# The hand-written schedule of a state-space mixer with a mixture of experts: x's scaling and z one unit later, x's stores earlier in the queue, and a new order inside chunk 0

## What is computed

```python
def layernorm(x): return (x - mean(x)) / sqrt(var(x) + 1e-5)

u  = layernorm(x)                                  # 16 x 512 x 128
h  = causal_convolution(u @ B_w.T, powers of eig)  # 64 states, |eig| = 1
x  = x + layernorm(h @ C_w.T + D * u)              # the mixer
t  = layernorm(x)
cw = softmax(t @ w_router) * softmax(t @ w_gating / 0.1); cw /= sum(cw) + 1e-9
o  = sum over 8 experts e of cw[e] * ((silu(t @ w_gate[e]) * (t @ w_up[e])) @ w_down[e])
x  = x + layernorm(o)
```

## Time and profile before

| | us |
|---|---|
| median of 3 runs | 1149.61 (1148.16 to 1149.87) |
| the profiled execution | 1147.37 |
| its span, first to last instruction | 1145.4 |
| PE busy | 1110.9 (97%) |
| DVE busy | 936.1 (82%) |
| ACT busy | 731.6 (64%) |
| POOL busy | 708.5 (62%) |
| TensorE clock granted, mean | 0.997 |

### The profile page before, as it was taken

How to read it: one execution, slowest core, us unless ns; L and a number is a source line. 1 busy time by engine, 2 the same in 40 slices (tenths; PEclk the granted TensorE clock), 3 DMA queues, 4 the chain that set the end, 5 groups by cost and what they waited for, 6 DMA issues and landing times.

```text
span 1145.4 us, 16858 instructions
## 1 busy us (share of the span) xinstructions
PE 1110.9 (97%) x4818; PEld 897.2 (78%) x4818; DVE 936.1 (82%) x1751; ACT 731.6 (64%) x1415; POOL 708.5 (62%) x900
## 2 busy tenths in 40 slices
PE   8998999999999999999999999999999999999997
PEld 4676787787877878787887877878777887888885
DVE  7778888787888978888887887978878887887865
ACT  6765666656666576666656666576666756666564
POOL 1587766648557475766748567575756748557453
PEclk9999999999999999999999999999999999999998
DMA  4430322213132222322213133222322313132110
GB/s 137 118 111 12 100 56 77 72 47 93 47 93 75 65 65 50 99 56 77 72 48 98 42 93 74 66 65 54 95 56 76 73 47 93 46 84 56 43 52 19
DMA packets 184588, 80.17 MB, mean 70 GB/s; under 512 B 126736, under 2 KB 162224, under 8 KB 184496
## 3 DMA queue, kind: packets, MB, share of 16 engines
q1 hardware_dynamic: 184496, 79.09, 26.2%
HBM read 59.40 MB, written 19.66 MB: 69 GB/s over the span
## 4 chain that ended last, share of the span: by engine, by line
PE 73%; POOL 14%; issue 7%; ACT 1%; DVE 1%; POOLq 0%; ACTq 0%; DVEq 0%
PE y L365 8%; PE g L367 8%; PE g L365 8%; PE g L366 8%; PE y L367 8%; PE y L366 8%; PE u L365 8%; PE u L367 7%; PE u L366 7%; POOL hid_lo L1285 6%; POOL acc L1292 2%; POOL mv L1236 1%; POOL rstd L1250 1%; ACT hid_hi L673 1%; PE m_ps L365 1%
## 5 line engine op out<-in xcount | busy, mean ns | idle before, releaser
L1285 POOL TENSOR_TENSOR hid_lo<-hid,hid_hi 128x512 fp32r<-128x512 f32 x255 | 335.3, 1315 | 363.5 <-ACT hid_hi L673 363.4
L983 DVE TENSOR_TENSOR hid<-gate,u 128x512 f32<-128x512 f32 x512 | 348.9, 682 | 188.6 <-ACT gate L667 163.9
L667 ACT ACTIVATE gate<-g 128x512 f32<-128x512 f32 x512 | 305.2, 596 | 299.2 <-PE g L367 298.9
L673 ACT ACTIVATE hid_hi<-hid 128x512 fp32r<-128x512 f32 x512 | 319.8, 625 | 38.3 <-DVE hid L983 36.4
L989 DVE TENSOR_TENSOR hid_lo<-hid,hid_hi 128x512 fp32r<-128x512 f32 x257 | 236.7, 921 | 0.1
L365 PE MATMUL y<-hid_hi,w_hi 128*128 128x512 f32 x512 | 201.6, 394 | 12.2 <-POOL hid_lo L1285 11.6
L365 PE MATMUL g<-xe_hi,w_hi 128*128 128x512 f32 x512 | 200.2, 391 | 4.5 <-POOL w_lo L1228 2.9
L365 PE MATMUL u<-xe_hi,w_hi 128*128 128x512 f32 x512 | 200.0, 391 | 2.4 <-DVE hid L983 2.4
L367 PE MATMUL g<-xe_hi,w_lo 128*128 128x512 f32 x512 | 199.4, 389 | 0.0
L367 PE MATMUL u<-xe_hi,w_lo 128*128 128x512 f32 x512 | 199.4, 389 | 0.0
L367 PE MATMUL y<-hid_hi,w_lo 128*128 128x512 f32 x512 | 199.4, 389 | 0.0
(11 more groups left out here) (223 smaller groups left out, 1165.1 us busy)
## 6 DMA issues: line engine op xcount, KB each, us to landing
cw_b<-cw_scratch SPq DMA_DIRECT2D x128, 256.0 KB, 3.4
x_sb<-x_in SPq DMA_DIRECT2D x16, 256.0 KB, 3.1
xn_scratch<-mix_t SPq DMA_DIRECT2D x60, 64.0 KB, 2.7
feat<-xn_scratch SPq DMA_DIRECT2D x15, 256.0 KB, 2.6
out_scratch<-acc_t SPq DMA_DIRECT2D x60, 64.0 KB, 1.9
ffn<-out_scratch SPq DMA_DIRECT2D x15, 256.0 KB, 2.7
x_out<-o_sb SPq DMA_DIRECT2D x15, 256.0 KB, 2.4
y_scratch<-mix_t SPq DMA_DIRECT2D x56, 64.0 KB, 1.9
```

Of the source, the lines that this page charges most:

```text
L667: nc.scalar.activation(gate[:, k % 2, :], g_ps[k % 2][:], ACT.Silu).then_inc(gate_ready, 1)
L673: nc.scalar.activation(hid_hi[:, k % RING, :], hid[:, k % RING, :], ACT.Copy).then_inc(hi_ready, 1)
L983: nc.vector.tensor_tensor(hid[:, k % RING, :], gate[:, k % 2, :], u_ps[k % 2][:], ALU.mult).then_inc(hid_ready, 1)
L1285: nc.gpsimd.tensor_tensor(hid_lo[:, k % RING, :], hid[:, k % RING, :], hid_hi[:, k % RING, :].bitcast(f32), ALU.subtract).then_inc(lo_pool, 1)
```

## The change

In every chunk from 1 on, `scale_x` and `z` move one unit down, and with them `residual`, `hi_x`, `du` and `lo_x`; `bu` and what follows stay. SP stores and loads x's blocks after expert 4's row instead of after expert 5's. In chunk 0 x of chunk 1 is turned by PE (four transposes into `n_ps`) instead of by DVE and two trips through DRAM, so that mixing starts 3 to 4 units earlier; chunk 0's own softmax steps are spread over units 1 to 6; the pieces of experts 4 to 7 are split 2 to 3 units earlier; chunk 1's softmax ends inside chunk 0.

```diff
-X_AT = {"load_x": 0, "stats_x": 4, "norm_x": 5, "scale_x_a": 7, "scale_x_b": 8, "block_x": 10, "hi_x": 15, "du": 16,
-        "lo_x": 16, "bu": 18, "enter": 19, "scan": 21, "leave": 22, "hi_w": 24, "lo_w": 25, "c": 27, "y": 28, "block_y": 30}
-Y_AT = {"stats_y": 6, "norm_y": 7, "z_a": 9, "z_b": 10, "residual": 11, "stats_x1": 14, "norm_x1": 15, "scale_x1_a": 18,
+X_AT = {"load_x": 0, "stats_x": 4, "norm_x": 5, "scale_x_a": 8, "scale_x_b": 9, "block_x": 10, "hi_x": 16, "du": 17,
+        "lo_x": 17, "bu": 18, "enter": 19, "scan": 21, "leave": 22, "hi_w": 24, "lo_w": 25, "c": 27, "y": 28, "block_y": 30}
+Y_AT = {"stats_y": 6, "norm_y": 7, "z_a": 10, "z_b": 11, "residual": 12, "stats_x1": 14, "norm_x1": 15, "scale_x1_a": 18,
...
-FIRST_X_AT = {"scale_x_a": 0, "scale_x_b": 1, "block_x": 1, "hi_x": 7, "du": 8, "lo_x": 8, "bu": 10, "enter": 11, "scan": 11,
-              "leave": 13, "hi_w": 14, "lo_w": 14, "c": 16, "y": 17}
+FIRST_X_AT = {"scale_x_a": 0, "scale_x_b": 1, "turn_x": 3, "hi_x": 4, "du": 4, "lo_x": 4, "bu": 6, "enter": 7, "scan": 7,
+              "leave": 9, "hi_w": 10, "lo_w": 10, "c": 12, "y": 13}
...
-LATE_SPLITS = (5, 7, 9, 11, 13, 15, 17, 18, 19, 21, 23, 25)
+LATE_SPLITS = (3, 4, 6, 8, 10, 12, 14, 16, 17, 18, 20, 22)
...
-                    if e == 5 and c + 2 < NCHUNK:
+                    if e == 4 and c + 2 < NCHUNK:
                         store_x_blocks(c + 2)
                         load_x_feat(c + 2)
...
+            def first_turn_x():
+                pe.wait_ge(xn_ready, 2)
+                pe.wait_ge(raw_read, 1)
+                turn(n_ps, lambda j: xn[:, j, :]).then_inc(xn_turned, 1)
...
-                nc.scalar.activation(act_hi[:], feat[:], ACT.Copy).then_inc(act_hi_ready, 1)
+                src = n_ps if c == 1 else feat
+                nc.scalar.activation(act_hi[:], src[:], ACT.Copy).then_inc(act_hi_ready, 1)
```

More of the change, by code:

```diff
@@ L47 @@
+Y_AT = {"stats_y": 6, "norm_y": 7, "z_a": 10, "z_b": 11, "residual": 12, "stats_x1": 14, "norm_x1": 15, "scale_x1_a": 18,
         "scale_x1_b": 19, "block_xe": 20, "hi_xe": 25, "lo_xe": 26, "logits": 28, "softmax": 29, "peak": 30, "silus": 31}
-FIRST_X_AT = {"scale_x_a": 0, "scale_x_b": 1, "block_x": 1, "hi_x": 7, "du": 8, "lo_x": 8, "bu": 10, "enter": 11, "scan": 11,
-              "leave": 13, "hi_w": 14, "lo_w": 14, "c": 16, "y": 17}
-FIRST_Y_AT = {"turn_y": 17, "stats_y": 17, "norm_y": 18, "z_a": 20, "z_b": 21, "residual": 22, "stats_x1": 23, "norm_x1": 24,
-              "scale_x1_a": 26, "scale_x1_b": 27, "turn_xe": 28, "hi_xe": 28, "lo_xe": 28, "logits": 29, "softmax": 30,
-              "peak": 31}
@@ L53 @@
-SECOND_X_AT = {"stats_x": 5, "norm_x": 6, "scale_x_a": 9, "scale_x_b": 10, "block_x": 12, "hi_x": 19, "du": 20, "lo_x": 20,
-               "bu": 21, "enter": 22, "scan": 22, "leave": 23, "hi_w": 25, "lo_w": 26, "c": 28, "y": 29, "block_y": 30}
+FIRST_X_AT = {"scale_x_a": 0, "scale_x_b": 1, "turn_x": 3, "hi_x": 4, "du": 4, "lo_x": 4, "bu": 6, "enter": 7, "scan": 7,
+              "leave": 9, "hi_w": 10, "lo_w": 10, "c": 12, "y": 13}
+FIRST_Y_AT = {"turn_y": 14, "stats_y": 14, "norm_y": 15, "z_a": 17, "z_b": 18, "residual": 19, "stats_x1": 20, "norm_x1": 21,
+              "scale_x1_a": 24, "scale_x1_b": 25, "turn_xe": 26, "hi_xe": 27, "lo_xe": 27, "logits": 28, "softmax": 29,
+              "peak": 30, "silus": 31}
@@ L55 @@
+SECOND_X_AT = {"stats_x": 5, "norm_x": 6, "scale_x_a": 9, "scale_x_b": 10, "block_x": 12, "hi_x": 18, "du": 19, "lo_x": 19,
+               "bu": 20, "enter": 21, "scan": 22, "leave": 23, "hi_w": 25, "lo_w": 26, "c": 28, "y": 29, "block_y": 30}
 OWN_AT = {"exps": 0, "products": 1, "weights": 2}
-FIRST_OWN_AT = {"exps": 1, "products": 1, "weights": 2}
+FIRST_OWN_AT = {"softmax": 1, "peak": 2, "silus": 3, "exps": 4, "products": 5, "weights": 6, "weigh": 10}
 FIN_AT = {"fin_turn": 7, "fin_stats": 12, "fin_norm": 13, "fin_a": 21, "fin_b": 22, "fin_add": 23}
@@ L267, in store_x_blocks @@
             def store_x_blocks(c):
-                sp.wait_ge(x_blocked, c)
-                if c > 1:
-                    sp.wait_ge(xt_loaded, 16 * (c - 1))
+                sp.wait_ge(x_blocked, c - 1)
+                if c > 2:
+                    sp.wait_ge(xt_loaded, 16 * (c - 2))
                 to_features(xn_dram, mix_t, x_stored)
             def load_x_feat(c):
-                sp.wait_ge(x_stored, STORED * c)
-                if c > 1:
+                sp.wait_ge(x_stored, STORED * (c - 1))
+                if c > 2:
                     sp.wait_ge(act_lo_ready, 2 * c - 3)
@@ L325, in body @@
                     load_x(c + 2)
-                if first:
-                    store_x_blocks(1)
                 store_cw(c, par)
-                if first:
-                    load_x_feat(1)
                 for e in range(E):
@@ L436, in mix_c @@
                 exact(m_ps[:], proj_hi[:, P:P + D], proj_lo[:, P:P + D], act_hi[:], act_lo[:]).then_inc(mixed_ready, 1)
+            def first_turn_x():
+                pe.wait_ge(xn_ready, 2)
+                pe.wait_ge(raw_read, 1)
+                turn(n_ps, lambda j: xn[:, j, :]).then_inc(xn_turned, 1)
             def first_turn_y():
                 pe.wait_ge(y_ready, 2)
-                pe.wait_ge(raw_read, 1)
                 turn(n_ps, lambda j: y_sb[:, j * P:(j + 1) * P]).then_inc(y_turned, 1)
@@ L530, in body @@
                             mix_c(m)
+                        if k == at.get("turn_x"):
+                            first_turn_x()
                         if k == at.get("turn_y"):
@@ L591, in mix_scale_x @@
                     if c == 2:
-                        act.wait_ge(x_blocked, 1)
+                        act.wait_ge(xn_turned, 2)
                 for j in tiles:
@@ L599, in mix_hi_x @@
             def mix_hi_x(c):
-                act.wait_ge(xt_loaded, 16 * c)
+                if c == 1:
+                    act.wait_ge(xn_turned, 2)
+                else:
+                    act.wait_ge(xt_loaded, 16 * (c - 1))
                 act.wait_ge(mixed_ready, c)
-                nc.scalar.activation(act_hi[:], feat[:], ACT.Copy).then_inc(act_hi_ready, 1)
+                src = n_ps if c == 1 else feat
+                nc.scalar.activation(act_hi[:], src[:], ACT.Copy).then_inc(act_hi_ready, 1)
             def mix_du(c):
@@ L608, in mix_du @@
                     act.wait_ge(y_blocked, c - 2)
-                nc.scalar.activation(y_sb[:], feat[:], ACT.Copy, scale=d_col[:]).then_inc(du_ready, 1)
+                src = n_ps if c == 1 else feat
+                nc.scalar.activation(y_sb[:], src[:], ACT.Copy, scale=d_col[:]).then_inc(du_ready, 1)
             def mix_hi_w(c):
@@ L630, in mix_scale_x1 @@
                     if 0 < c < NCHUNK - 1:
-                        act.wait_ge(x_blocked, c + 1)
+                        act.wait_ge(x_blocked, c)
                 for j in tiles:
@@ L718, in body @@
                         round_piece(n // PIECES, n % PIECES)
-                    if first and k == 1:
+                    if first and k == FIRST_OWN_AT["silus"]:
                         mix_silus(0)
-                    if c == 1 and k == 0:
-                        mix_silus(1)
                     for m, at in stages(c):
@@ L817, in block_x @@
                 dve.wait_ge(xn_ready, c + 1)
-                if c > 1:
-                    dve.wait_ge(x_stored, STORED * (c - 1))
+                if c > 2:
+                    dve.wait_ge(x_stored, STORED * (c - 2))
                 if c > 2:
@@ L825, in block_y @@
                 dve.wait_ge(y_ready, c + 1)
-                dve.wait_ge(x_stored, STORED * c)
+                dve.wait_ge(x_stored, STORED * (c - 1))
                 nc.vector.transpose(mix_t[:], y_sb[:]).then_inc(y_blocked, 1)
@@ L837, in mix_lo_x @@
                 dve.wait_ge(act_hi_ready, 2 * c - 1)
-                nc.vector.tensor_tensor(act_lo[:], feat[:], act_hi[:].bitcast(f32), ALU.subtract).then_inc(act_lo_ready, 1)
+                if c == 1:
+                    dve.wait_ge(du_ready, 2)
+                src = n_ps if c == 1 else feat
+                nc.vector.tensor_tensor(act_lo[:], src[:], act_hi[:].bitcast(f32), ALU.subtract).then_inc(act_lo_ready, 1)
             def mix_enter(c):
                 dve.wait_ge(bu_ready, c + 1)
+                if c == 1:
+                    dve.wait_ge(cw_t_ready, 1)
                 nc.vector.tensor_tensor(v_sb[:], m_ps[:], trig[:], ALU.mult).then_inc(mix_link, 1)
@@ L1136, in body @@
                         hid_low(c - 1, UNITS - 1, False)
-                    if first and k == 0:
+                    own = FIRST_OWN_AT if first else OWN_AT
+                    if k == own.get("softmax"):
                         mix_softmax_in(0)
+                    if k == own.get("peak"):
                         mix_peak(0)
-                    own = FIRST_OWN_AT if first else OWN_AT
                     if k == own["exps"]:
@@ L1146, in body @@
                         mix_weights(c)
```

(4 more changed lines are left out.)

## The result

The changed kernel is slower: 1173.76 us median of four runs (1172.01 to 1175.31), beside 1149.74 for the kernel before on the same chip; ratio 1.0208, 95% interval 1.0186 to 1.0231 (the ratios below are to the kernel before too, with the same kind of interval). The forecast was 1172.5. The profiled execution took 1172.01, 24.6 more than that of before (1147.37); its span is 1170.1.

A forecast was written before the change was run, and what follows sets the result against it. PE, busy 97%, was taken to bound the kernel through its stops. 15.1 + 18.2 - 6.15 - 4.2 = +22.95 took the profiled 1147.37 to 1170.3; 2.24 carried over gave 1172.5 us. Range 1166 to 1179; 8 in 10: 1154 to 1179.

The forecast's parts named there:

- step 1: Steady chunks, x's scaling and z on ACT moved one unit down: costs nothing, covered by ACT's idle time.
- step 2: Residual on POOL behind add_part makes hid_lo of unit 13 late for PE: 1.08 us in 14 chunks, 15.1.
- step 3: lo_x on DVE waits its turn at the port behind POOL's add_part, delaying bu: 1.4 us in 13 chunks, 18.2.
- step 4: x's stores leave 4 us earlier, hi_x stands a unit later: ACT's wait for feat goes, gaining 6.15 us.
- The stop in unit 8: Steady chunks, PE's y waits for POOL's hid_lo behind norm_x; nothing moves it. Rival that it goes: 1159.2, 5%.
- Chunk 0, 4.2: Chunk 0: two stops gone, 3.1 and 1.5, less 0.45 for PE's new turn_x: gain 4.2 us.
- Both named stops: Chunk 0, PE before unit 28 for w_lo (3.1 with restart) and y before turn_y (1.5): both go.
- the rest stays in size, at other places: Chunk 0: the remaining 5.3 us of PE's standing, from DVE's and POOL's full units, stays but moves.
- its bounds: Chunk 0's gain: 0 if hid_lo behind the earlier norm_x1 is late instead; 9.4 if every stop went.
- only the residual is felt: Rival, steady chunks: lo_x escapes as DVE's hid_low goes ahead or add_part comes late; 1154.4, 12%.
- POOL absorbs the residual: Rival, faster: POOL's stretch from unit 11 to 16 absorbs the residual and lo_x meets no queue; 1139.3, 8%.
- A norm's power: POOL's norm power (1.02 us) would, by the rule, hold off DVE, hid_lo 0.4 later, 5.6 over 14 chunks; not summed.

The follow-up runs named there:

- the last two kernels: Changed kernel with residual 11, lo_x 16, then norms moved later, residual 12, fin_norm 18: 1127.84 us; that plus norm_x1 22, bu 21, last split behind unit 24: 1124.06.
- the experiment with the last recurrent stop taken away: Changed kernel with residual 11 and lo_x 16, then norm_x 5 to 7, norm_y 7 to 8, residual 12, fin_norm 13 to 18: 1127.84 us.
- the other two kernels: Changed kernel with residual 11, lo_x 16, norm_x1 22, bu 21: 1140.46 us; that with norms moved later and chunk 0's last split behind unit 24: 1124.06.
- lo_x back: Changed kernel with lo_x put back from unit 17 to 16, everything else kept: 1158.52 us, ratio 1.0084 to the kernel before.
- both back: Changed kernel with lo_x put back to unit 16 and residual to unit 11: 1141.28 us, ratio 0.9935 to the kernel before.

## Why the prediction was right

Point by point, with chunk 3's times from its start.

- **x's scaling and z (step 1), nothing:** no wait of ACT or DVE for them is in the trace, and the undisturbed chunk is 68.23 with and without them. Held.
- **The residual (step 2), 1.08 us in 14 chunks:** hid_lo of unit 13 was to start at 34.6 and starts at 34.58; PE's y stands 0.94 longer than usual (284.08 to 285.25 is 1.17, 0.23 is usual), the matmul behind it comes 0.08 later than usual, together 1.02 for the forecast 1.08, and chunk 14 is 1.01 longer. Put back, it gives 0.85 beside the other stop and 1.24 alone. The mechanism came out in each link: the 0.45 at the port moved from the norm's first instruction to the residual, and the norm behind it took 2.77 (281.06 to 283.83).
- **lo_x (step 3), 1.4 us in 13 chunks:** it was to be issued at 40.3 and end at 42.1, and does at 40.27 and 42.04. The stop at bu is 1.33 over the usual plus 0.08, the forecast's own terms; put back, it gives 1.18 beside the other stop and 1.57 alone. That it is the place behind add_part at the port is shown by the run that moved add_part.
- **The sum of both:** 2.48 a chunk forecast, 2.42 measured (70.65 - 68.23).
- **The queue (step 4), 6.15:** 6.5 by the stretches of the run with that line alone. The stop in unit 8 stayed, as said.
- **Chunk 0, 4.2: the term that was mis-sized.** It measured 1.2 in the trace. Both named stops went as said (3.33 and 1.75 start to start before; none, and 0.56), but "the rest stays in size, at other places" was wrong: without the two named stops PE stood 5.0 in chunk 0 before and stands 7.7 now, above all before y of unit 24 (2.87 from start to start, hid_lo behind norm_x1) and before bu (1.71). The prediction named the reason among its bounds (POOL's load unchanged, hid_lo behind the earlier norm_x1) and gave it no weight. The earlier trace rows had the mean only, 56.29 of 77.56 for POOL. A stretch of 20 us in the kernel before shows it, 18.73 of 20 (same columns; from 80 to 100 it is 19.37):

```profile
71.73:91.73 20.00, 18.88 (x82) 14.65 (x82) 14.61 (x24) 12.70 (x25) 18.73 (x20) 1.00 0.21 65
```

The errors partly cancel: 0.8 less in the steady stops (32.5 for 33.3), 0.4 more from the queue, 3.0 less from chunk 0, so +24.8 by the trace for +22.95. That the 3.0 did not matter is the size of the steady terms, not the reasoning on chunk 0. The 2.24 from the profiled execution to the median, carried over from before, came out at 1.75.

- **The rivals:** "only the residual is felt" and "POOL absorbs the residual" each fall by the waits, m_ps behind act_lo 14 times and y behind hid_lo 28 times (I had said about 32; five of the 18 before were late feat's, and went with it, and chunk 0 has a new one). In the last two kernels the residual in unit 12 is in fact absorbed, with fin_norm out of that stretch.
- **A norm's power did not hold DVE off.** In the changed kernel's chunk 3 DVE's hid_low began inside the power (282.51 to 283.53) and took its 0.68, and hid_lo of unit 13 came at 34.58, not 0.4 later than 34.6. The rule of the Trainium skill, page "SBUF — State Buffer", section "Who interferes with whom", has the shared pair held for the whole instruction; the trace differs from it for the power, and agrees for two instructions of 128x512: lo_x took 1.77, the rest of add_part and its own time.

```profile
282.51 1.02 POOL L1282 TENSOR_TENSOR rstd<-var_eps,half 128x4 f32<-128x4 f32 x1
...
283.13 0.68 DVE L999 TENSOR_TENSOR hid_lo<-hid,hid_hi 128x512 fp32r<-128x512 f32 x1
```

## What to carry over

Before a step is moved by a unit, add up what the engine does between the two outputs that another engine waits for, and see how much is to spare: here 0.36 us decided over some 14 us of the total, and a 1.29 us instruction moved two rows down took it. A stretch's mean share hides that; take it in pieces of a few units and look for the one without a gap. And test a schedule change by its parts: this one held 6.5 us of gain from a single line, buried under some 32 us of loss from two numbers.

## What the runs showed that I had not expected

**A long stop can cost the clock.** In the experiment with the last recurrent stop taken away, PE stands 3.13 from start to start before y of unit 24, and behind it matmuls run at 0.43 from start to start instead of 0.23:

```profile
91.44 0.47 PE L361 MATMUL y<-hid_hi,w_hi 128*128 128x512 f32 x1 [2.74 <-POOL hid_lo L1298]
...
92.65 0.63 PE L362 MATMUL g<-xe_lo,w_hi 128*128 128x512 f32 x1
93.07 0.63 PE L363 MATMUL g<-xe_hi,w_lo 128*128 128x512 f32 x1
...
95.62 0.39 PE L363 MATMUL y<-hid_hi,w_lo 128*128 128x512 f32 x1
```

```profile
92.65:96.00 3.35, 3.35 (x10) 2.67 (x9) 0.92 (x2) 2.26 (x5) 2.35 (x2) 0.56 0.02 5
```

The granted clock is 0.56 on the mean over those 3.35 us, for the most part the lower of its two levels, 1.2 GHz, and full again behind them. Chunk 0 took 78.15 there, 1.8 more than in the changed kernel, of which 0.26 is a longer stop. Nine profiles have a stop of 2.86 or more in chunk 0, and three lost the clock behind it: this one, the kernel with the queue's line alone (stop 3.33, chunk 0 79.21) and the one with add_part moved (stop 2.86, chunk 0 77.95). The kernel before with the same 3.33, three kernels with 3.12 or 3.13, and two with 2.87, the changed kernel among them, did not. Behind the shorter stops in chunk 0 of the other two kernels (2.33 and 1.73 at most) it did not fall either. The length of the stop alone doesn't decide: in two more profiles, "lo_x back" and "both back", the clock fell ahead of chunk 0, behind a stop of 1.99 that all eleven profiles have near 29.4, and chunk 0 begins at 32.5 and 32.6 there, at 31.5 to 31.9 in the others. What decides is open. In "both back":

```profile
30.00:32.00 2.00, 2.00 (x6) 1.16 (x5) 0.84 (x2) 1.08 (x3) 1.38 (x3) 0.50 0.43 128
```

So a stop of some 3 us cost 1.5 to 1.7 us beyond itself, in some executions and not in others: the kernel before and the one with the queue's line alone run the same program in chunk 0, and one of the two lost it. The runs without a profile fit that. Of the 15 runs of the kernel before beside the queue's experiment, the three with a mean granted clock of 0.994 took 1150.21 to 1150.96 and the three with 0.998 took 1147.58 to 1148.25. Such a stop is worth removing first.
